# Earlier normalization, another order of the opening products, and the last residual rows summed in the accumulator's place

## What is computed

```python
x = x + attn(layernorm(x))
x = x + ffn(layernorm(x))

q, k, v = ((h @ w.T + b).reshape(B, S, 32, 32) for each)
scores = einsum('bshd,bstd->bsht', q, k) / sqrt(32)
context = einsum('bsht,bstd->bshd', softmax(scores), v)

# ffn: w1, w2 (2752 x 1024) and w3 (1024 x 2752) are first rounded to the
# 16 NF4 levels, scaled by the largest absolute value of each 64 weights
h = silu(x @ dq1.T) * (x @ dq2.T)
out = h @ dq3.T
```

## Time and profile before

| | us |
|---|---|
| median of 3 runs | 1895.01 |
| lowest, highest | 1889.67, 1895.59 |
| the profiled execution | 1894.59 |
| its span | 1892.7 |
| PE busy | 1831.2 (97%) |
| DVE busy | 1729.0 (91%) |
| ACT busy | 1378.0 (73%) |
| POOL busy | 1252.9 (66%) |

### The profile page before, as it was taken

The page is one execution under the profiler, slowest core; times in us unless marked ns, Lnnn a source line. Parts: engine busy times, 40 slices in busy tenths (PEclk is TensorE's granted clock), DMA queues, the critical chain, the costliest instruction groups (busy, mean ns, idle before and its releaser), DMA issues. The chain is left out here.

```text
span 1892.7 us, 42748 instructions
## 1 busy us (share of the span) xinstructions
PE 1831.2 (97%) x16470; PEld 884.2 (47%) x16470; DVE 1729.0 (91%) x1848; ACT 1378.0 (73%) x1523; POOL 1252.9 (66%) x706
## 2 busy tenths in 40 slices
PE   6899999999989999999999999999999999999998
PEld 6555555555434344444444444444444444444443
DVE  6799999999888999999999999999999999999985
ACT  7233333333359898898998988989989889898881
POOL 0134534534647887977878779778787787787961
PEclk9999999999999999999999999999999999999999
DMA  9346666665587131221122212212211221131115
GB/s 322 123 128 188 169 173 198 170 174 157 133 215 239 41 66 45 45 62 49 44 52 47 56 44 50 61 44 50 61 44 44 50 61 44 44 65 42 39 29 190
DMA packets 252925, 182.76 MB, mean 97 GB/s; under 512 B 177792, under 2 KB 220800, under 8 KB 252800
## 3 DMA queue, kind: packets, MB, share of 16 engines
q1 hardware_dynamic: 221600, 167.28, 31.8%
q10 hardware_dynamic: 31200, 13.64, 3.5%
HBM read 114.29 MB, written 24.12 MB: 73 GB/s over the span
## 5 line engine op out<-in xcount | busy, mean ns | idle before, releaser
L1718 DVE SCALAR_TENSOR_TENSOR bank<-signs,bank 128x1024 f32<-128x1024 int8 (+2 forms) x756 | 919.9, 1217 | 53.2 <-ACT signs L1584 25.8
L1878 PE MATMUL bank<-x2T,w12T 128*128 128x512 f16 x4128 | 896.3, 380 | 8.3 <-DMA x2T<-x_lo_dram 5.9
L1878 PEld LDWEIGHTS bank<-x2T,w12T 128*128 128x128 f16 x4128 | 403.9, 98 | 497.5 <-DMA x2T<-x_lo_dram 6.4
L1584 ACT ACTIVATE signs<-w_first,compare_bias 128x1024 int8<-128x1024 f32 (+1 forms) x588 | 630.6, 1138 | 1.5 <-DVE bank L1718 1.1
L1584 ACT ACTIVATE signs<-w_last,compare_bias 128x1024 int8<-128x1024 f32 (+2 forms) x294 | 314.4, 1119 | 0.8 <-DVE w_first L1718 0.6
L1068 PE MATMUL bank<-wT,xT_hi 128*128 128x512 f16 x768 | 294.8, 384 | 2.4 <-PEq L321 2.4
L1068 PE MATMUL bank<-wT,xT_lo 128*128 128x512 f16 x768 | 294.1, 383 | 2.0 <-issue 2.0
L1906 PE MATMUL bank<-w3T_hi,hT_hi 128*128 128x512 f16 x672 | 255.3, 380 | 7.5 <-DMA w3T_lo<-half 4.7
L1907 PE MATMUL bank<-w3T_lo,hT_hi 128*128 128x512 f16 x672 | 255.4, 380 | 0.0
L1908 PE MATMUL bank<-w3T_hi,hT_lo 128*128 128x512 f16 x672 | 255.4, 380 | 0.0
L1498 POOL TENSOR_TENSOR acc<-acc,hidden 128x512 f32<-128x512 f32 x160 | 201.1, 1274 | 27.5 <-ACT hidden L1625 26.7
(11 more groups left out here) (140 smaller groups left out, 2142.7 us busy)
## 6 DMA issues: line engine op xcount, KB each, us to landing
ff_raw<-in_L_ffn_w SPq DMA_DIRECT2D x63, 512.0 KB, 4.6
w_first<-in_L_ffn_w SPq DMA_DIRECT2D x41, 512.0 KB, 3.8
w_last<-in_L_ffn_w SPq DMA_DIRECT2D x19, 512.0 KB, 4.0
x_nat<-in_L_attn_hidden_states SPq DMA_DIRECT2D x16, 512.0 KB, 5.8
x_res<-in_L_attn_hidden_states SPq DMA_DIRECT2D x16, 512.0 KB, 5.3
x<-x_res SPq DMA_DIRECT2D x16, 512.0 KB, 3.6
acc<-x SPq DMA_DIRECT2D x4, 2048.0 KB, 8.2
out<-acc SPq DMA_DIRECT2D x15, 512.0 KB, 2.6
```

What stands on the lines that cost most here:

```text
L1584: nc.scalar.activation(signs[0:rows, ring(v, k), 0:cols], w_nat(v % SLOTS)[0:rows, 0:cols], ACT.Sign, scale=COMPARE[SUMMED[k]][0], bias=co ...
L1718: V.scalar_tensor_tensor(to, part, HALF_STEP[SUMMED[k]], total, ALU.mult, ALU.add).then_inc(sign_used, 1)
L1878: last = nc.tensor.matmul(dst, w, tokens_of(sb_, x)[:, :, c], start=c == 0 and i == 0, stop=c == C - 1 and i == 2)
```

## The change

It has these parts. (1) DVE's `norm_apply` stands ahead of `center(n, 0)` instead of behind it, in every step that has both. (2) PE spreads the feed-forward scales (L1927) behind the first 64 x 2 score products of step 15, not at the end of step 14. (3) The second and third of PE's four opening passes change places: up part of block 0, then gate of block 1. (4) For tiles 14 and 15 the residual rows are loaded early, straight into `acc[:, 14]` and `acc[:, 15]`, summed there by POOL, and never stored to x1 or loaded back; `norm2` reads them there, writes `x_res`, and waits for the turns of the tile before instead of for the store. Both loads are issued in step 15 once the scales have been spread, since their place in SBUF is that of `ff_raw`; small fillers in SBUF set the place.

The core of the diff (left out are the fillers and the dictionary that passes the names on):

```diff
@@ -249,7 +249,10 @@
             sp.dma_start(x_nat[:, slot], x_dram[bass.ds(n * P, P), :]).then_inc(x_in[slot], 16)
 
         def load_res(sp, n):
-            sp.dma_start(x_res[:], x_dram[bass.ds(n * P, P), :]).then_inc(res_in, 16)
+            sp.dma_start(sum_rows_of(n), x_dram[bass.ds(n * P, P), :]).then_inc(res_in, 16)
+
+        def sum_rows_of(n):
+            return shared["acc"][:, n] if isinstance(n, int) and n >= T - 2 else x_res[:]
 
         def moments(dve, rows, part, mv, ve, ready, scale=1.0):
 
@@ -669,6 +674,9 @@
                     sp.wait_ge(x_turned, 2 * n + 2)
                     load_x(sp, n + 2, u)
                 if feed:
+                    next(feed)
+                    for last in (T - 2, T - 1):
+                        load_res(sp, last)
                     sp.wait_ge(projected, 6 * n + 2)
                     next(feed)
                     turn_high2(sp, n - 2)
@@ -680,7 +688,7 @@
                     sp.sem_inc(held, 1)
                 for look in todo[4:]:
                     load_ff(*look)
-                if end and attend:
+                if end and attend and not feed:
                     load_res(sp, n - 1)
                 if feed:
                     next(feed)
@@ -699,20 +707,15 @@
 
             def tail(feed):
                 sp.wait_ge(projected, 6 * T)
-                store_x1(T - 2)
                 next(feed)
-                sp.wait_ge(x2_turned, 32 * (T - 1))
-                sp.sem_inc(held, 1)
-                load_res(sp, T - 1)
                 next(feed)
-                store_x1(T - 1)
                 next(feed)
 
             sp.wait_ge(w_turned, GROUPS * PAIRS)
             load_res(sp, 0)
             sp.sem_inc(x2_out, 32)
             all_steps(sp, step, tail, feed)
-            sp.wait_ge(x1_out, 16 * T)
+            sp.wait_ge(x1_out, 16 * (T - 2))
             sp.wait_ge(x2_out, 32 * (T - 1))
 
         def gpsimd(pool, feed):
@@ -761,8 +764,8 @@
 
             def residual(n):
                 pool.wait_ge(ctx_ready, n + 1)
-                pool.wait_ge(res_in, 16 * (n + 1))
-                rows = x_res[:].rearrange("p (h u d) -> p h u d", u=2, d=HD)
+                pool.wait_ge(res_in, 16 * T if isinstance(n, int) and n >= T - 2 else 16 * (n + 1))
+                rows = sum_rows_of(n).rearrange("p (h u d) -> p h u d", u=2, d=HD)
                 nc.gpsimd.tensor_tensor(rows, rows, flipped[:].rearrange("p (h d u) -> p h u d", d=HD, u=2), ALU.add).then_inc(res_done, 1)
 
             def inv_std2(n):
@@ -837,12 +840,12 @@
                     look()
                 if project:
                     evacuate(n, u, it, 0, 0)
+                if normalize and attend:
+                    norm_apply(dve, n + 1, 1 - u)
                 if attend:
                     center(n, 0)
                 if feed:
                     next(feed)
-                if normalize and attend:
-                    norm_apply(dve, n + 1, 1 - u)
                 look()
                 if attend:
                     flip_probs(n, 0, end)
@@ -925,7 +928,7 @@
 
             def moments2(n):
                 dve.wait_ge(res_done, n + 1)
-                moments(dve, x_res[:], stats2, mean_var2, var_eps2, var2_ready, X_SCALE)
+                moments(dve, sum_rows_of(n), stats2, mean_var2, var_eps2, var2_ready, X_SCALE)
 
             def center(n, half):
 
@@ -938,8 +941,11 @@
 
             def norm2(n):
                 dve.wait_ge(rstd2_ready, n + 1)
-                dve.wait_ge(x1_out, 16 * (n + 1))
-                nc.vector.tensor_scalar(x_res[:], x_res[:], mean_var2[:, 0:1], rstd2[:, 0:1],
+                if isinstance(n, int) and n >= T - 2:
+                    dve.wait_ge(x2_turned, 32 * n)
+                else:
+                    dve.wait_ge(x1_out, 16 * (n + 1))
+                nc.vector.tensor_scalar(x_res[:], sum_rows_of(n), mean_var2[:, 0:1], rstd2[:, 0:1],
                                         ALU.subtract, ALU.mult).then_inc(normed2, 1)
 
             def flip_probs(n, half, end):
@@ -1084,6 +1090,8 @@
                     pe.wait_ge(x_lo_done, 2 * n + 2)
                     if attend:
                         score_part(n, end, 0, HALF)
+                    if feed:
+                        next(feed)
                     project_one(n, u, it, 0, with_lo, score_second if attend else None)
                 if normalize:
                     pe.wait_ge(normed, n + 2)
@@ -1093,8 +1101,6 @@
                     if attend:
                         mix_part(n, HALF, QUAD)
                     project_one(n, u, it, 2, with_lo, ahead_half if ahead else None)
-                if ahead:
-                    next(ahead)
 
             def score_part(n, end, first, last):
 
@@ -1207,8 +1213,8 @@
         hT_hi = sb("hT_hi", [P, 2, SB * BANK], F16)
         hidden = sb("hidden", [P, 2, BANK])
         hT_lo = sb("hT_lo", [P, 2, SB * BANK], F16)
-        acc = sb("acc", [P, T, E])
-        sb("apart", [P, 16])
+        acc = shared["acc"] = sb("acc", [P, T, E])
+        sb("apart", [P, 24])
         x2T_first = sb("x2T0", [P, ST_BLOCK, 2, C, P], F16)
 
 
@@ -1384,10 +1390,10 @@
                         load_acc(3, SB)
 
             def load_acc(first, last):
-                sp.wait_ge(x1_out, 16 * T)
+                sp.wait_ge(x1_out, 16 * (T - 2))
                 sp.wait_ge(x2_turned, 32 * T)
                 for b in range(first, last):
-                    tiles = slice(b * ST_BLOCK, (b + 1) * ST_BLOCK)
+                    tiles = slice(b * ST_BLOCK, min((b + 1) * ST_BLOCK, T - 2))
                     sp.dma_start(acc[:, tiles], x1_dram.rearrange("(t p) e -> p t e", p=P)[:, tiles]).then_inc(acc_in[b], 16)
 
             def load_tokens(b, count=ST_BLOCK):
@@ -1415,6 +1421,8 @@
             for slot in range(SLOTS):
                 sp.sem_inc(w_in[slot], 16)
             load_tokens(0)
+            yield
+            sp.wait_ge(tops_spread, 1)
             yield
             load(0, 3, P)
             sp.wait_ge(x2_turned, 32 * (T - 3))
@@ -1570,6 +1578,7 @@
             pool.wait_ge(inv_ready, 3)
             pool.wait_ge(scaled, 1)
             yield
+            pool.wait_ge(shared["res_done"], T)
             rounds(pool, body)
 
         def scalar(act):
@@ -1911,7 +1920,7 @@
             def body(r, sizes, opening=False):
                 for w in range(4):
                     if opening and w == 0:
-                        for at, (m, sb_) in enumerate(((0, 0), (0, 1), (1, 0), (1, 1))):
+                        for at, (m, sb_) in enumerate(((0, 0), (1, 0), (0, 1), (1, 1))):
                             gate_up(r, 0, sb_, P, (m,), True, 3 * C * at)
                         continue
                     gate_up(r, w // 2, w % 2 * 2, sizes[w // 2], opening=opening)
```

More of the change, by code:

```diff
@@ L520, in attention @@
         ff_raw = sb("ff_raw", [P, 2, E])
+        sb("past_rows", [P, 8])
         stats2 = sb("stats2", [P, 2, 6])
@@ L563, in attention @@
         PROJ_RING = 4
+        shared = {}
         mixing = bank[:, 4:6].rearrange("p b n -> p (b n)")
@@ L1157, in tensor @@
                 whole_program(step_with_lo)
-        shared = {"ff_raw": ff_raw, "x1_out": x1_out, "x2_out": x2_out, "projected": projected, "evacuated": evacuated, "ctx_read": ctx_read,
+        shared |= {"ff_raw": ff_raw, "res_done": res_done, "x1_out": x1_out, "x2_out": x2_out, "projected": projected, "evacuated": evacuated, "ctx_read": ctx_read,
                   "x2_turned": x2_turned, "x2_hi_done": x2_hi_done, "x2_lo_done": x2_lo_done, "x2_half": x2_half, "x2_low": x2_low,
```

## The result

The changed kernel takes 1917.38 us (median of 4, 1914.83 to 1917.94), the kernel before 1893.61 (median of 4 beside it, 1889.67 to 1895.59). The ratio is 1.0126, with the 95% interval 1.0105 to 1.0146: some 24 us slower, where 9 were forecast and 1908 was the upper end.

A forecast was written before the change was run, and what follows sets the result against it. TensorE bounds the feed-forward rounds, so their start decides; in the loop neither engine bounds alone. Loop +8.8, spread 0 and turn +0.5 make +9.3 us on the profiled 1894.6: 1904, own range 1900 to 1908, whole range 1889.5 to 1908.

The forecast's parts named there:

- What bounds, and what moves to the end: Feed-forward rounds: TensorE is busy throughout, so time the earlier stages hand to it comes out at the end one for one.
- If L760 comes first, L275 lasts ... 2.77 us instead of 1.45: Attention loop: VectorE's normalization stands until GpSimd's addition ends, making VectorE 1.32 us late in each of ten steps.
- A: Rival, loop: in odd steps the normalization starts before GpSimd's addition and takes 0.80 us; 1892 in all, chance 0.22.
- B: Rival, loop: the normalization starts before GpSimd's addition in all steps, TensorE gets rows early; 1890 in all, chance 0.08.
- Loop: 13.2 - 9.8 + 5.4 = +8.8: Loop: 13.2 us extra VectorE time, less 9.8 of its old waits for TensorE, plus 5.4 of waits left.
- TensorE's own fetch gaps come on top (three of 2.9 us in all at the mixing): Loop: the fetch gaps counted when walking the steps to find VectorE's remaining 5.4 us of waits.
- with one more [fall] 10.5: Loop: its loss in us if TensorE's clock falls once more than assumed; 5.8 without any fall.
- the walk: Following the engines' waits step by step; in the loop it left 5.4 us of waits, giving +8.8 us.
- The spread of the scales: 0.: Step 15: TensorE's 2.7 us wait shrinks by 1.3, but it waits later for probabilities; 0, bounds 0 and +1.
- L942 then stands at 531.8, inside GpSimd's L1465, and would end 0.55 behind it: Turn: norm2 without its store wait is blocked by a GpSimd operation and comes 2.4 us earlier, not 4.05.
- [Block 1's gate] ends at 546.5 ... Turn: +0.5: Turn: the late gate delays ScalarE's second silu and signs, using up the 2.4 us; +0.5, bounds -2.4 and +1.5.
- Rival C: Turn: ScalarE isn't held by the second silu, VectorE's 2.4 us reach the last tile; 1898 to 1901.5, chance 0.13.

The follow-up runs named there:

- e3: e1 with GpSimd's first level addition of a step waiting until the normalization is done; 1890.81 us, 0.9977 of the kernel before.
- e15: As e1, with GpSimd's two-input addition L760 replaced by a one-input `is_gt, mult`; 1905.74 us, 1.0063 of the kernel before.
- e1: The kernel before with only norm_apply moved ahead of center in steps 1 to 14; 1911.38 us, 1.0099.
- e10: The changed kernel with the loop's ff_raw loads cut to 32 bytes per row instead of 4 KB; 1905.59 us, 1.0056 of the kernel before.
- e11: The kernel before with the loop's ff_raw loads cut to 32 bytes per row instead of 4 KB; 1888.75 us, 0.9963.
- e6: The kernel before with only the sums in the accumulator's place and the later spread of the scales; 1892.22 us, 0.9988.
- e12: e2 with ScalarE's four opening comparisons put ahead of the second silu; 1892.15 us, 0.9984 of the kernel before.
- e2: The changed kernel with norm_apply back behind center, its other parts kept; 1898.98 us, 1.0030 of the kernel before.
- e5: The kernel before with only the second and third opening passes swapped; 1900.75 us, 1.0037.
- e14: As e1, with GpSimd's two-input addition L760 replaced by a one-input `mult, add`; 1896.12 us, 1.0009 of the kernel before.
- e7: The changed kernel with GpSimd's first level addition of a step waiting for the normalization; 1895.48 us, 1.0006 of the kernel before.

## Why the prediction was wrong

- **What bounds, and what moves to the end**: right. The rounds are unchanged; the last landing moves by 22.8 us and the span by 23.2.
- **"If L760 comes first, L275 lasts ... 2.77 us instead of 1.45"**: right, in nine of ten steps, 0.01 us of lead included; A and B are out. e3 shows what the block is worth: 21 to 23 us. The Trainium skill's "SBUF — State Buffer", section "Who interferes with whom", has the same rule for a VectorE instruction in a two-port mode: whoever issues first keeps the shared ports, and the other blocks. That the lock lasts for the whole instruction, as it says, doesn't fit e15, where L275 ends 1.58 us after the start of an operation of 3.63 us; the measurement decides.
- **"Loop: 13.2 - 9.8 + 5.4 = +8.8"**: the step that failed. VectorE's extra work was about right, 11.6 us for 13.2 (nine steps, not ten). Of its waits for TensorE 5.4 us were to be left, and 16.4 are; its waits for `ff_raw`, put at nothing without a reason, grew by 2.0. That is 11.6 - 9.8 + 16.4 + 2.0 = 20.2, the measured 20.1. The 5.4 came from a walk in which "TensorE's own fetch gaps come on top (three of 2.9 us in all at the mixing)". It took the gaps as fixed and counted three of the eight; they were 8.6 us and became 19.2, with four falls of the clock behind them, and "with one more [fall] 10.5" was too small a bound. e1 measures +19 (16 to 22) for this part. With the transfers cut in both kernels (e10, e11) the stretch loses 9.1 in place of 20.1, near the walk's 8.8, though by other terms (14.5 of work, 5.0 less of waits). So the transfers make some half of the loop's loss in the traces; by the ratios they make 6 of the 24 us, give or take 5.
- **The spread of the scales: 0.** Not tried alone. TensorE's wait for the mix shrank from 2.7 to 1.4 us, as said; e6 bounds it, since spread and sums together give -2.
- **"L942 then stands at 531.8, inside GpSimd's L1465, and would end 0.55 behind it"**: wrong in the mechanism, right in the number by luck. L948 starts 1.68 us into L1473 and takes 0.80; e15 shows that the blocking part is then over. The 4.05 us were cut to 2.5 by the exponential that stood behind three comparisons (1.56), where 2.4 was written.
- **"[Block 1's gate] ends at 546.5 ... Turn: +0.5"**: the mechanism is right (e12), the size is not: e2 +6, e5 +7. The step that failed here: the walk "It does 16 (3.5 us) and meets the first mixing ... plus 16 products" had no fetch gap in the mixing and the slow clock only as a bound. e5 shows 4.37 us and 5.41 for 16 products, so the second silu comes 8.4 us behind the first, where 1.1 to 2.6 were written. Rival C was out for the reason given.
- The sum of the parts by ratio, 18.8 (e1) - 2.3 (e6) + 7.0 (e5) = 23.5, is near the measured 23.9.

What stays open: why the fetch gaps grow with the new order (8.6 to 19.2 us; 12.7 in e3, 17.4 in e14, but 8.1 in e7), and why the gap of step 13 doesn't shrink without the loads (other transfers, such as the transposes and stores of x2, go on).

## What to carry to other kernels

Before a short VectorE operation is moved, look at who starts within a few hundredths of a microsecond on GpSimd: e3's one wait turned +19 us into -4. Where TensorE's program has "issue" gaps at places that recur, another order in the loop can change their length, and cutting the transfers shortened them; a forecast needs a bound with several of them at 3 to 4 us and a fall of the clock behind. When passes are swapped on one engine, follow the in-order engine that takes their results: four comparisons behind a late silu cost 7 to 9 us.

## What the runs showed of the hardware

- GpSimd's `is_gt, mult` on 128x1024 float32 takes 3.63 us and holds VectorE's TENSOR_SCALAR (0.80 us alone), which then ends 1.58 us after its start (e15); `mult, add` takes 1.04 us and holds it just as long (e14). One that came 1.68 us into the longer one wasn't held (0.80 us, changed kernel).
- Most of TensorE's fetch gaps come behind the same product in several kernels of this program (the 111th score product of step 7: 0.43, 1.27, 3.01 and 3.29 us in e10, before, e1 and after). They are longer beside data transfers: 54 loads cut from 512 to 4 KB took away 16 of 19 us (e10).
